# Rows in tiles of 256, 256, 512, 512 and 512 instead of four of 512, gathers up to a ring's length ahead, products folded by DMA in 42 rounds and by VectorE in 18

## The reference

```
z[b, pair(i, j)] = sum over d of (e[b, i] @ w[pair])[d] * e[b, j][d]
h = relu(concat(z, dense_ctx[b]) @ W_top1 + b_top1)      # 512 -> 512
h = relu(h @ W_top2 + b_top2)                            # 512 -> 256
y = h @ W_top3                                           # 256 -> 1
```

## Time and profile before

| | |
|---|---|
| median of 3 runs | 859.3 us (859.05 to 859.55) |
| span of the profiled execution | 856.9 us; its own time is not listed apart from the runs |
| TensorE busy | 782.8 us (91%) |
| VectorE busy | 592.4 us (69%), 512 instructions |
| ScalarE busy | 195.7 us (23%) |
| GpSimd busy | 574.1 us (67%), 512 gathers and 81 folds |
| mean granted clock of TensorE | 0.980 of 2.4 GHz |

### The profile page before, as it was taken

One profiled execution on the slowest core, in us unless ns is written; L12 is line 12 of the kernel. 1 busy time (PEld: TensorE's weight loads), 2 busy tenths in 40 slices (PEclk: granted clock), 3 DMA queues, 4 the chain that ended last, 5 costly groups with the idle time before them and its releaser, 6 DMA issues.

```text
span 856.9 us, 10445 instructions
## 1 busy us (share of the span) xinstructions
PE 782.8 (91%) x3912; PEld 287.9 (34%) x3912; DVE 592.4 (69%) x512; ACT 195.7 (23%) x333; POOL 574.1 (67%) x597
## 2 busy tenths in 40 slices
PE   0467739998989999999999999999999999999998
PEld 0122213333333333333333333333333333333333
DVE  0145528977877768868689677877788677887750
ACT  1222202131222132311322222311322223200002
POOL 6777775778777777777787777777777777710100
PEclk9969969999999999999999999999999999999999
DMA  4524539969797887888697986888786988994820
GB/s 131 203 52 100 122 78 197 218 156 200 167 199 166 182 187 158 191 181 173 152 203 157 204 182 139 196 184 182 140 204 161 200 195 189 193 187 92 167 56 0
DMA packets 38601, 138.07 MB, mean 161 GB/s; under 512 B 11092, under 2 KB 11476, under 8 KB 28056
## 3 DMA queue, kind: packets, MB, share of 16 engines
q0 software_dynamic: 28048, 101.75, 60.3%
q1 hardware_dynamic: 10504, 35.67, 12.2%
HBM read 52.43 MB, written 0.01 MB: 61 GB/s over the span
## 4 chain that ended last, share of the span: by engine, by line
PE 76%; POOL 13%; issue 5%; DMA 5%; DVE 1%; ACT 0%; POOLq 0%; DVEq 0%
PE main_ps L332 44%; PE z_ps L355 17%; POOL emb L233 12%; PE x_ps L386 8%; PE x_ps L312 4%; DMA prod<-prod 4%; PE main_ps L386 2%; POOL prod L245 1%; DMA emb<-in_tbl,idx 1%; DVE prod L419 1%; PE main_ps L333 1%; ACT quad_t L442 0%; DMA idx<-in_ids 0%; ACT y_sb L465 0%; POOLq L230 0%
## 5 line engine op out<-in xcount | busy, mean ns | idle before, releaser
L419 DVE TENSOR_TENSOR prod<-main_ps,quad_t 128x1024 f32<-128x1024 f32 x448 | 521.8, 1217 | 151.8 <-PE main_ps L333 151.3
L233 POOL DMA_INDIRECT emb<-in_tbl,idx x512 | 494.0, 965 | 165.4 <-issue 149.2
L332 PE MATMUL main_ps<-e_t,w_sb 64*128 64x512 f32 x1024 | 488.6, 617 | 4.1 <-ACT e_t L431 4.1
L333 PE MATMUL main_ps<-e_t,w_sb 64*128 64x512 f32 x1024 | 488.6, 617 | 0.0
L332 PEld LDWEIGHTS main_ps<-e_t,w_sb 64*128 64x128 f32 x1024 | 185.0, 191 | 260.8 <-issue 184.3
L355 PE MATMUL z_ps<-prod,const_sb 128*32 128x512 f32 x1400 | 177.4, 604 | 28.3 <-DMA prod<-prod 26.1
L333 PEld LDWEIGHTS main_ps<-e_t,w_sb 64*128 64x128 f32 x1024 | 185.0, 191 | 0.0
L419 DVE TENSOR_TENSOR prod<-main_ps,e_t 128x1024 f32<-128x1024 f32 x64 | 78.1, 1220 | 83.8 <-PE main_ps L333 83.8
L442 ACT ACTIVATE quad_t<-x_ps 32x512 f32<-32x512 f32 x224 | 131.2, 586 | 2.7
L245 POOL DMA_DIRECT2D prod<-prod x81 | 80.0, 993 | 74.0 <-DVE prod L419 69.3
L431 ACT ACTIVATE e_t<-x_ps 128x512 f32<-128x512 f32 x64 | 38.2, 597 | 400.0 <-PE x_ps L312 400.0
(11 more groups left out here) (11 smaller groups left out, 24.3 us busy)
## 6 DMA issues: line engine op xcount, KB each, us to landing
prod<-prod POOLq DMA_DIRECT2D x81, 1024.0 KB
w_sb<-in_w SPq DMA_DIRECT2D x65, 512.0 KB, 5.8
emb<-in_tbl,idx POOLq DMA_INDIRECT x512
w_sb<-in_w SPq DMA_DIRECT2D x1, 1024.0 KB, 11.9
z_sb<-in_ctx SPq DMA_DIRECT2D x64, 2.0 KB
idx<-in_ids SPq DMA_DIRECT2D x1, 192.0 KB, 9.6
const_sb<-in_const SPq DMA_DIRECT2D x1, 125.0 KB, 2.2
idx<-in_ids SPq DMA_DIRECT2D x1, 64.0 KB, 1.9
```

What stands on the lines that cost most here:

```text
L233: pool.indirect_dma_start(out=emb[:, n % G_SLOTS, s, odd * EMBED:(odd + 1) * EMBED], out_offset=None, in_=tables[f], in_offset=bass.Indire ...
L332: nc.tensor.matmul(main_ps[:, slot, :], w_sb[LOW, u % W_SLOTS, :], even[LOW, 0, :], start=True, stop=True)
L333: nc.tensor.matmul(main_ps[:, slot + 1, :], w_sb[UP, u % W_SLOTS, :], odd[UP, 0, :], start=True, stop=True)\
L419: nc.vector.tensor_tensor(prod[:, s:s + 2, :], main_ps[:, slot:slot + 2, :], e_q, ALU.mult)\
```

## The change

- *Tiles.* The batch goes as five tiles of 256, 256, 512, 512 and 512 rows. In a half tile a duo has 4 gathers and 2 transposes. Two groups of units share a round, one in each half of the columns, so a half tile has 16 rounds. A *step* is what VectorE multiplies at once: a unit of 512 columns, or two units of 256 (lines 481, 482, 598).
- *Units.* The eight "duo" and eight "twin" units of a tile give way to four "star" groups of three units each (`star_units`), which need operands mixed from two duos: ScalarE makes them (`mix_quad`, four copies for each quad, into four more slots of `e_t`). A tile has 124 units instead of 128. Star units are multiplied from `e_t` (line 581).
- *Gathers.* The ring has 12 halves (the same memory). Up to round 32 of all, and by a fixed count behind it (`gathers_before`), GpSimd issues gathers as far ahead as the ring allows.
- *Folds.* None in the half tiles and in the first 20 rounds of tile 2, but for VectorE's. 42 rounds are folded by DMA. 18 rounds, six in each full tile, those before a round with an MLP step, are folded by an addition of VectorE (line 604).
- *Weights* are loaded once for each of five tiles, 80 loads; `W_top1` in one order of rows for half tiles and one for full ones. The MLP of a half tile has 256 columns.

```diff
-TILE = 512
-def ahead(n):
-
-    return 2 if n < 10 else 3 if n < DUOS else G_SLOTS
-POOL_GATHERS = 4
+FULL, HALF = 512, 256
+WIDTHS = (HALF, HALF, FULL, FULL, FULL)
+G_HALVES = 12
+def order_groups():
+    low = []
+    for m in range(13, 1, -1):
+        low += [(m, q) for q in range(QUADS - 1, m // 2, -1)]
+    low += [(m, q) for q in range(QUADS - 1, 0, -1) for m in (1, 0)]
+    groups = [("low", low[k:k + 2]) for k in range(0, len(low), 2)]
+    for at, q in ((2, 7), (7, 5), (18, 3), (29, 1)):
+        groups.insert(at, ("star", (q, q - 1)))
+    return groups
+def star_units(qa, qb):
+
+    a, b = [4 * qa + k for k in range(4)], [4 * qb + k for k in range(4)]
+    return [((a[2], (a[0], a[1])), (a[1], (a[0], a[3]))),
+            ((b[0], (b[2], b[3])), (b[1], (b[0], b[3]))),
+            ((b[2], (b[1], b[3])), (a[3], (a[0], a[2])))]
+def steps_of(t, r):
+
+    if WIDTHS[t] == FULL:
+        return [(r, (p,)) for p in range(4 if GROUPS[r][0] == "low" else 3)]
+    return [(g, (j, j + 2) if GROUPS[g][0] == "low" or j == 0 else (j,)) for g in (2 * r, 2 * r + 1) for j in range(2)]
+MLP_AT = {1: (4, 5, 7, 9, 11, 12, 13)} | {t: (6, 10, 14, 18, 22, 26, 30) for t in (2, 3, 4)}
+
+V_FOLDS = [(t, r) for t in (2, 3, 4) for r in (n - 1 for n in MLP_AT[t]) if foldable(t, r)]
+UNFOLDED = {0: range(16), 1: range(16), 2: range(20), 3: (0, 11, 16, 23, 27), 4: (3, 11, 16, 23, 30, 31)}
+FOLDS = [(t, r) for t, r in ROUNDS if foldable(t, r) and r not in UNFOLDED[t] and (t, r) not in V_FOLDS]
+STEADY = (-9, -7, -5, -3, -1, 1, 3, 5, 7, 9, 11, 13, 15, 17, 19, 21)
+DUO_AT = {1: (-4, -3, -2, -1, -1, 0, 1, 2, 3, 4, 5, 6, 7, 8, 9, 10), 2: (-5, -4, -2, -1, 0, 2, 3, 5, 7, 9, 11, 13, 15, 17, 19, 21),
+          3: STEADY, 4: STEADY}
+            n = max(FIRST_DUO[t][m] - 1, 0) if t == 0 else min(STEP0[ROUND0[t] + DUO_AT[t][j]], FIRST_DUO[t][m])
+            lead = (2 if WIDTHS[t] == FULL else 0) + q % 2
+                put(STEP0[ROUND0[t] + r] + (2 if WIDTHS[t] == HALF else 0), ("mlp", t - 1, n))
+FREE_ROUNDS, FIVES = 32, 52
+def gathers_before(G):
+    return 170 + 5 * (min(G, FIVES) + 1 - FREE_ROUNDS) + 4 * max(G - FIVES, 0)
...
-                if n >= ahead(n) and k == 0:
-
-                    pool.wait_ge(transposed, n - ahead(n) + 1)
+                if BEFORE[n] >= 0 and k == 0:
+
+                    pool.wait_ge(transposed, BEFORE[n] + 1)
...
+                if (t, r) in V_FOLDS and n + 1 == STEP0[G + 1]:
+
+                    dve.wait_ge(products, n + 1)
+                    a = prod_tile(G, 0, 0)
+                    nc.vector.tensor_tensor(prod[:, a:a + 4, :], prod[:, a:a + 4, :], prod[:, a + 4:a + 8, :], ALU.add).then_inc(v_folded, 1)
...
+            def mix_quad(t, q):
+                first, pair = q % 2 == 1, q if q % 2 else q + 1
+                act.wait_ge(evicted, EVICTED["duo", t, 2 * q])
...
+                nc.scalar.activation(one[LOW, :], a[LOW, :], ACT.Copy)
+                nc.scalar.activation(one[UP, :], b[UP, :], ACT.Copy)
```

More of the change, by code:

```diff
@@ L43 @@
[L43 to L64, removed]
@@ new lines, in main_products @@
+                if n >= MAIN:
+                    pe.wait_ge(products, n - MAIN + 1)
+                slot = 2 * (n % MAIN)
+                for h, p in enumerate(ps):
+                    kind, what = GROUPS[g]
+                    u = (NGROUP * SLOTS4 * t + SLOTS4 * g + p) % W_SLOTS
+                    if kind == "low":
+                        low = up = what[p % 2][0]
+                    else:
+                        low, up = (side[0] // 2 for side in star_units(*what)[p])
+                    c = slice(HALF * h, HALF * h + WIDTHS[t])
+                    nc.tensor.matmul(main_ps[:, slot, c], w_sb[LOW, u, :], e_duo(t, low)[LOW, :], start=True, stop=True)
+                    last = nc.tensor.matmul(main_ps[:, slot + 1, c], w_sb[UP, u, :], e_duo(t, up)[UP, :], start=True, stop=True)
@@ new lines, in main_products, with reduce_round @@
+                last.then_inc(mains, 1)
+            def reduce_round(G):
+                t, r = ROUNDS[G]
+                k, rr = divmod(r, ROUNDS_KT)
+                if rr == 0 and Z0[t] + k > 0:
+                    pe.wait_ge(z_out, Z0[t] + k)
+                pe.wait_ge(products, STEP0[G + 1])
+                folded = (t, r) in FOLDS or (t, r) in V_FOLDS
+                if (t, r) in V_FOLDS:
+                    pe.wait_ge(v_folded, V_FOLDS.index((t, r)) + 1)
+                elif folded:
@@ new lines, in reduce_round @@
+                if len(set(kinds)) == 1:
+                    spans = [(kinds[0], slice(0, FULL))]
+                else:
+                    spans = [(kind, slice(HALF * c, HALF * c + HALF)) for c, kind in enumerate(kinds)]
+                todo = []
+                for p in range(2 if folded else 4):
+                    for kind, c in spans:
+                        if kind == "low" or p < 3:
+                            todo += [(p, x, kind, c) for x in range(2)]
+                for i, (p, x, kind, c) in enumerate(todo):
+                    q = 2 * (p % 2) + x
+                    if kind == "low":
+                        lhs = sel_quad[:, 28 - 4 * rr:60 - 4 * rr]
+                    else:
+                        s = 2 * rr + (p >= 2)
+                        lhs = sel_duo[:, 30 - 2 * s:62 - 2 * s]
+                    final = not any(2 * (pp % 2) + xx == q for pp, xx, _, _ in todo[i + 1:])
+                    last = nc.tensor.matmul(z_ps[32 * q:32 * q + 32, c], lhs, prod[:, prod_tile(G, p, x), c],
+                                            start=(rr == 0 and p < 2), stop=(rr == ROUNDS_KT - 1 and final))
@@ L424, in keep_duo @@
             def keep_duo(t, m):
+                width = WIDTHS[t]
                 act.wait_ge(transposed, duo_number(t, m) + 1)
[L426 to L431 removed]
+                j = DUOS - 1 - m
+                if width == FULL and j >= E_SLOTS:
+                    act.wait_ge(products, FINAL_DUO[t][m + E_SLOTS] + 1)
+                elif t:
+                    slot = e_place(t, m)[0]
+                    before = (slot + E_SLOTS,) if WIDTHS[t - 1] == FULL else (2 * slot, 2 * slot + 1)
+                    act.wait_ge(products, max(FINAL_DUO[t - 1][DUOS - 1 - b] for b in before) + 1)
+                last = nc.scalar.activation(e_duo(t, m), x_ps[:, 0:width], ACT.Copy)
                 q = m // 2
```

573 lines of the change are left out of this document (334 added, 239 removed).

## The result

The change runs in 840.99 us (median of 4 runs, 839.39 to 841.97), the kernel before beside it in 859.21 (859.05 to 859.55): ratio 0.9785, 95% interval 0.9773 to 0.9797. It is faster, by 18.2 us where 38 were forecast: 20 us above the forecast, at the high end of the range. The profiled execution spans 840.1 us.

A forecast was written before the change was run, and what follows sets the result against it. TensorE was taken as the bound, starved in the first tile by gathers, then by folds. Its work of 807.0 us plus 12 of stalls made 819.0; with 2.4 around the span, 821 us, range 809 to 841.

The forecast's parts named there:

- the mechanism of the ramp: First tile: 4 gathers a duo and first fold behind gather 275 end the fold stalls; tile 0 ends at 122.2 us.
- the 807.0 us of work: Whole kernel: TensorE's work without stalls, summed from the start to step 15, five tiles and the tail.
- 12 us of stalls: Whole kernel: four stalls that the change adds, 2, 5, 3 and 2 us, on top of TensorE's work.
- step 15: First tile: transposes of duo 7 wait for gathers until 50.2 us, step 15 runs at 50.7, no gather waits behind it.
- tail: Behind the last tile: 825.88 to 856.9 us of the kernel before stays as it is, 31.0 us.
- Stall (1): Ramp: first steps at 1.2 GHz and one more clock dip at waits before steps 7 and 10; 2 us, 0 to 5.
- Stall (2): Tile 1: MLP steps and half duos wait for the shared bank `x_ps`; 5 us, between 3 and 8.
- Stall (3): Tiles 2 and 3: GpSimd's folds late by some 5 us, with 3 of slack; 3 us, between 0 and 10.
- rival B: GpSimd becomes the bound, each VectorE addition holding it for 2.3 us: +14, 835 us; chance 0.12.
- Stall (4): A half tile's star rounds: VectorE waits for mixes, from the reductions' order; 2 us, between 0 and 4.
- A: Half-width passes don't hide their loads: 0.19 us added to each of 496 passes, 94 us, 915 us; chance 0.05.
- C: Half width costs more than half: passes at 0.232, half activations at full price, longer cold start: 837 us; chance 0.11.

The follow-up runs named there:

- the pieces: The change with each VectorE addition cut in four pieces of 512 columns: 836.48 us, ratio 0.9732 to the kernel before.
- three repairs: The change with additions in four pieces, duos and mixes spread out in the second half tile, and last star group at place 23: 827.84 us.
- four small repairs: The change with split additions, spread duos and mixes, star group at 23, and last two MLP steps of the first half tile one step later: 825.92 us.
- the second sample of the change: The change run once more, unaltered: 840.14 us, ratio 0.9774 to the kernel before.

## Why the prediction was wrong

The direction and the mechanism of the ramp were right; the size was off by half. The step that failed is what I added to the 807.0 us of work: 12 us of stalls, where the change takes 33. Of these 33, 2.4 lie ahead of step 15, 18.6 are waits behind it, 6.9 are slow passes behind waits and 3.2 are breaks that I had priced too low; some 2 are left over. The prediction and the trace of the change, split alike, are:

| stage | predicted | measured | over |
|---|---|---|---|
| step 15 runs | 50.7 | 53.1 | 2.4 |
| tile 0, from there | 71.5 | 76.0 | 4.5 |
| tile 1 | 104.5 | 115.5 | 11.0 |
| tile 2 | 183.4 | 186.3 | 2.9 |
| tile 3 | 185.3 | 191.2 | 5.9 |
| tile 4 | 180.6 | 184.5 | 3.9 |
| tail | 31.0 | 33.5 | 2.5 |

**The work without stalls: right but for the breaks.** Half width is half a pass, and the additions take 2.293 us (2.3 predicted). The version without additions has the full clock in tiles 0 to 4, so it shows the sums. Less its waits, tile 0 from step 15 on is 71.7 us (71.5 predicted), and tile 3 is 190.5, as much as six more whole rounds at 0.86 on 185.3 make. Too low was tile 1, 107.7 less its waits where I had 104.5. The breaks in a half tile's round are longer: 0.37 to 0.475 for a pair of transposes, not 0.3, and about 2.3 for a half MLP step in the middle of a round, not 1.92.

**Step 15:** late by 2.4. Before it TensorE waited 3.17 us for a gather, until 46.35, and the passes up to 49.27 started 0.42 apart.

**Stall (1), the clock:** 2 predicted, 6.9 measured from tile 0's end on, in the profiled run. Two dips stand right there. A clock of 0.83 over 10 us and of 0.89 over 32 is half speed for 3.4 and 7.0 us, so 5.2 us lost; another 1.7 lie behind the wait of 488.9. I priced waits, and not the slow passes that follow one of 2 us or more.

**Stall (2), the bank:** 5 predicted, 4.8 measured (0.57, 1.98, 1.17, 1.03 us), though at other places: I had not looked at the two duos in a row.

**Stall (3), folds:** 3 predicted (0 to 10), 8.7 measured, the largest miss of the four. Two things are in it. The hold of rival B, which I left out of the forecast, is worth 2.2 us: that is what the pieces gain in tiles 2 and 3. The rest stays with pieces (6.3 us). It falls to 1.7 us in the version without additions, where TensorE also gets 5 us more to do a tile, and to 3.6 in the one with three repairs. What I had wrong is GpSimd's slack. I compared whole tiles, 177 us of it with 185 of TensorE, but folds stand in a row. VectorE's products of rounds 27 and 28 of tile 2, and the issues of their folds:

```profile
406.85 9.24 DVE L588 TENSOR_TENSOR prod<-main_ps,quad_t 128x1024 f32<-128x1024 f32 x8 [0.48 <-PE main_ps L482]
```

```profile
415.06 1.02 POOL L365 DMA_DIRECT2D prod<-prod  x1
...
421.22 0.99 POOL L365 DMA_DIRECT2D prod<-prod  x1
```

Four gathers and a fold take GpSimd 6.16 us, these two rounds of products come 4.6 us apart, and GpSimd has no idle but the 0.30 before each gather. So the first fold is issued 3.6 us behind its last product, the second 5.1, and TensorE waits 1.11 us for that one. The lateness grows to 8.8 us in round 4 of tile 3 (468.67 against 459.87). There it is 7.2 us both without additions and with additions in pieces, so most of it comes from the gathers ahead of the folds, and not from the hold. A kernel with fewer gathers between these folds was not run.

**Stall (4), mixes:** 2 predicted, 2.81 in one wait, and the clock behind it.

**The tail:** that no wait is added was said without looking; it is 2.4 us, for the context's DMA.

**Rivals.** A is false: the pitch is 0.2155 with each load beside the passes. The Trainium skill (TensorE: Matmul & The Clock Gate, section on the mechanism of packing) says in its list of what overlaps that a load does so only where the row groups differ; at 256 columns, as at 512, the trace disagrees. The same section lets a load run ahead into a background weight buffer too, which would fit; no run here shows which it is. B's mechanism is there, and so is its sign, gathers longer than 1 us beside additions: its hold is 1.2 us an addition on average, not 2.3. It gives 2.2 us, not 14. C's passes are false, its half activations part true: copies and mixes at 256 columns take 0.37 to 0.42 where 512 take 0.59 to 0.63, two thirds and not half. That lengthens the time that ScalarE holds the bank and the mixes. ScalarE's copies into `quad_t`, grouped with shapes kept apart:

```profile
L630 ACT ACTIVATE quad_t<-x_ps 32x512 f32<-32x512 f32 x168 | 98.4, 586 | 2.0
L630 ACT ACTIVATE quad_t<-x_ps 32x256 f32<-32x256 f32 x112 | 41.7, 372 | 1.3
```

That 840.99 us lies inside the range, by 0.01, is luck: the high end of 841 was B or C with late folds, and neither made the 20 us. The first full tile begins at 247, not near 230.

**What the change did for its 18.2 us.** The one line that takes the folds out of the first tile gives 16.1 alone. The forecast had this as "the stalls for folds go", but counted the half tiles, the star units and the additions on top as if nothing would be given back. Next to that line, the change waits 8 us less for gathers (31.4 against 39.6), and with the repairs its halves are worth 10 us.

## What to carry to other kernels

A fold, a gather, any DMA issued from one queue is placed by what stands ahead of it, so a more generous look-ahead can make the kernel slower (842.75 to 853.71 us): count the issues ahead of the first one that is waited for. Work saved while an engine waits for a supply of fixed rate is worth nothing, and a new wait of 2 us may cost as much again in clock, or nothing. Try the smallest piece of a large change alone first; here one line had nearly all (842.75 us), and four small repairs of the rest brought 15 us more (825.92 us). An average over a tile hides a queue that is late: compare it round by round where its work bunches.

## What the runs showed of the hardware

- An addition of VectorE on two SBUF operands holds a GpSimd gather that starts beside it until 0.81 to 0.87 us after its end (up to 0.93 in the second sample of the change). In four pieces of 0.69 us the longest gather is 1.40 us instead of 3.04.
- Waits of 1.98 and 2.8 us left stretches at a granted clock of 0.83 and 0.89 in the change, and at 1.00 in a version with the same instructions there that reached them 1.4 us later. In two samples of one program a wait of 2.41 us had no low clock behind it and one of 2.50 us at the same place had (0.94 over 30.1 us).
- ScalarE's copies have a fixed part: 0.372 us at 256 columns against 0.586 at 512, so some 0.16 whatever the width, by an estimate from these two (2 x 0.372 less 0.586).
- A pass of 64 rows by 256 columns and its weight load of 0.19 us in 0.2155 us: the load is hidden wholly, with some 0.03 us to spare.
